# Grouped attention: the last two steps divide the probabilities before the product with the values, and the last output weights take another place and another time

## The reference, cut to what matters

```
q = rmsnorm((x @ q_proj.T) by head);  k = rmsnorm((ctx @ k_proj.T) by group);  v = ctx @ v_proj.T by group
scores = q @ k.T * scale + mask
attn = softmax(scores)            # exp(scores - max) / sum
out = (attn @ v) by head
x = x + out @ o_proj.T
```

## Time and profile before

| | |
|---|---|
| median of three runs | 867.71 us (864.17 to 871.29) |
| profiled execution | 866.43 us, of which the span from first to last instruction is 864.3 us |
| busy share of the span | PE 90%, DVE 83%, ACT 60%, POOL 48% |
| mean granted clock of PE | 0.974 |
| step 14 by PE's units | 711.5 to 744.5 us of the span |
| step 15 with its tail | 744.5 to 783.2 us |

### The profile page before, as it was taken

How to read it: one execution, slowest core, us unless ns; L and a number is a source line. 1 busy time by engine, 2 the same in 40 slices (tenths; PEclk the granted TensorE clock), 3 DMA queues, 4 the chain that set the end, 5 groups by cost and what they waited for, 6 DMA issues and landing times. The chain is left out here.

```text
span 864.3 us, 16319 instructions
## 1 busy us (share of the span) xinstructions
PE 779.7 (90%) x5146; PEld 631.4 (73%) x5146; DVE 715.1 (83%) x1743; ACT 522.2 (60%) x1414; POOL 415.8 (48%) x372
## 2 busy tenths in 40 slices
PE   1976799858988999999999999999999999788878
PEld 0475577534677898898898888888888888675446
DVE  7877998969787887887897897897897897787975
ACT  6875798745556657557557657657657556551521
POOL 3237068715036745845744845745746645511110
PEclk9998999979999999999999999999999999899989
DMA  8255236544020310310220220320220220003001
GB/s 300 101 164 155 73 123 229 173 126 149 26 74 21 119 35 20 97 54 3 94 73 0 97 73 0 97 73 0 97 73 0 74 75 1 26 1 119 0 1 49
DMA packets 37775, 66.20 MB, mean 77 GB/s; under 512 B 5537, under 2 KB 17889, under 8 KB 37602
## 3 DMA queue, kind: packets, MB, share of 16 engines
q1 hardware_dynamic: 37730, 65.63, 23.2%
HBM read 60.28 MB, written 5.34 MB: 76 GB/s over the span
## 5 line engine op out<-in xcount | busy, mean ns | idle before, releaser
L2377 DVE TENSOR_SCALAR_CACHE_REDUCE xn<-ctxT,candidate 128x512 bf16<-128x512 f32 x240 | 168.8, 741 | 0.0
L2029 ACT ACTIVATE layer_attention_probs<-xnT,stats 128x512 f32<-128x512 f32 x128 | 93.9, 734 | 123.2 <-DVE stats L2172 123.2
L1764 PE MATMUL bank<-layer_attention_keysT,layer_attention_queriesT 128*128 128x512 f32 x384 | 121.9, 426 | 5.0 <-DVE layer_attention_queriesT L2165 5.0
L2184 DVE TENSOR_TENSOR layer_attention_probsT<-bank,layer_attention_probsT 128x512 fp32r<-128x512 f32 x128 | 88.1, 688 | 44.7 <-ACT layer_attention_probsT L2037 43.2
L1764 PEld LDWEIGHTS bank<-layer_attention_probsT,layer_attention_values 128*128 128x128 f32 x768 | 99.6, 190 | 13.4 <-DVE layer_attention_probsT L2184 6.0
L1764 PE MATMUL bank<-layer_attention_probsT,layer_attention_values 128*128 128x256 f32 x768 | 102.4, 283 | 5.1 <-DVE layer_attention_probsT L2184 5.1
L2037 ACT CAST layer_attention_probsT<-bank 128x512 fp32r<-128x512 f32 x128 | 74.9, 585 | 52.3 <-PE bank L1840 48.4
L1764 PE MATMUL bank<-layer_attention_l_wq,layer_attention_xnT 128*128 128x512 f32 x384 | 93.5, 392 | 0.0
L1764 PEld LDWEIGHTS bank<-layer_attention_l_wkv,layer_context_parts 128*128 128x128 f32 x720 | 88.5, 188 | 2.8
L1764 PE MATMUL bank<-layer_attention_l_wkv,layer_context_parts 128*128 128x256 f32 x720 | 90.5, 278 | 0.0
L1764 PE MATMUL bank<-layer_attention_wo,layer_attention_headsT 128*128 128x512 f32 x336 | 88.8, 406 | 0.0
(11 more groups left out here) (338 smaller groups left out, 1717.7 us busy)
## 6 DMA issues: line engine op xcount, KB each, us to landing
layer_attention_l_raw_qo<-in_wqT SPq DMA_DIRECT2D x8, 1024.0 KB, 5.5
layer_attention_l_raw_qo<-in_woT SPq DMA_DIRECT2D x8, 1024.0 KB, 6.5
xnT<-inverse_sums SPq DMA_DIRECT2D x15, 512.0 KB, 3.8
tw_raw<-in_w_gateT SPq DMA_DIRECT2D x8, 688.0 KB, 5.2
tw_raw<-in_w_upT SPq DMA_DIRECT2D x8, 688.0 KB, 4.3
tw_raw<-in_w_downT SPq DMA_DIRECT2D x6, 768.0 KB, 4.7
layer_attention_l_raw_kv<-in_wkvT SPq DMA_DIRECT2D x8, 512.0 KB, 4.8
ternary<-tw_rounded SPq DMA_DIRECT2D x8, 344.0 KB, 2.5
```

The costliest lines, as they stand in the source:

```text
L1764: last = pe.matmul(out, stationary[f][a], moving[f][b], start=f == 0 and x == 0, stop=f == count - 1 and x == 2)
L2029: a.activation(probs[:, u % 3, :], masked[:, u % 2, :], ACT.Exp, bias=negmax[:, u:u + 1], scale=-1.0, accum_out=sums[:, u:u + 1]).then_inc ...
L2184: v.tensor_tensor(probsT[:, 1, p % 2, :, columns], T[u % 2][:, :].rearrange("p (c q) -> p c q", c=CPB), probsT[:, 0, p % 2, :, columns], A ...
L2377: own(k.nc.vector.tensor_scalar((k.flags if flags is None else flags)[:, r % 2], row_tile(k.ctxT, r), k.candidate[:, r:r + 1].bitcast(F32) ...
```

## The change

Step 14 is made like step 15: the sums are inverted by unit on DVE, ACT scales each unit's probabilities, and the heads are split by ACT and DVE; the spread through DRAM and POOL's scale_heads of step 14 are gone. The split heads of both steps and the last output weights take halves of the context parts (ctxT2) that no later product reads. The last output weights are split earlier: ACT's halves stand after u 3 and 4, and POOL's halves on either side of norm(15, KEYS), as in odd steps. In step 15 the output product of step 14 is spread in quarters over u 1, 3, 5 and 6, where it stood at u 4 and 5 in halves; the last product runs by row block over three heads, and the fourth head after the last mix. DVE's pieces of the choice and its additions move by a unit or so. The functions last_turn, last_mix, last_heads_high, last_heads_low and last_invert are merged into the general ones.

```diff
-    FINAL_PIECES = (1, 1, 1, 1, 1, 1, 1, 1)
+    FINAL_PIECES = (1, 2, 1, 2, 1, 1, 1, 1)
...
-        last_inverse = k.sbuf("last_inverse", [P, UNITS], F32, s)
-        last_headsT, last_wo = xnT2, wq
+        last_inverse = k.sbuf("last_inverse", [P, 2 * UNITS], F32, s)
+        last_wo = ctxT2[:, :, :, 0:D]
...
+        def divided(step):
+            return step[0] is None and step[1] >= STEPS - 2
+
+        def divided_heads(step):
+            return ctxT2[:, :, :, D + step[1] % 2 * SEQ:D + (step[1] % 2 + 1) * SEQ]
...
 sync:    run((None, STEPS - 3), weights=False)
-                run((None, STEPS - 2))
...
 gpsimd run():
-                    if odd:
+                    if odd or not weights:
                         o_weights_low(step, 0)
                     norm(following, own, KEYS)
-                    if odd:
+                    if odd or not weights:
                         o_weights_low(step, 1)
                     norm(following, own, 0)
...
-                    elif not odd:
-                        o_weights_low(step, 0)
-                        o_weights_low(step, 1)
...
-                for j in range(2):
-                    scale_heads((None, STEPS - 2), j)
...
 tensor, turn_probs():
-                    pe.wait_ge(S_["exp_ready"], at(step, UNITS, u + 1))
+                    if divided(step):
+                        pe.wait_ge(S_["probs_scaled"], divided_unit(step, u + 1))
+                    else:
+                        pe.wait_ge(S_["exp_ready"], at(step, UNITS, u + 1))
...
 tensor, run_final():
+                        if u == 1:
+                            project_out(before, 0, 0)
                         if u == 2:
-                            last_mix(0)
+                            mix(final, 0)
+                        if u == 3:
+                            project_out(before, 0, 1)
                         if u == 4:
-                            last_mix(1)
-                        if u in (4, 5):
-                            project_out(before, u - 4, 0)
-                            project_out(before, u - 4, 1)
+                            mix(final, 1)
+                        if u == 5:
+                            project_out(before, 1, 0)
                         if u == 6:
-                            last_mix(2)
-                    last_project_out(0)
-                    last_project_out(1)
-                    last_mix(3)
-                    last_project_out(2)
-                    last_project_out(3)
+                            mix(final, 2)
+                            project_out(before, 1, 1)
+                    last_project_out(0, (0, 1, 2))
+                    mix(final, 3)
+                    last_project_out(1, (0, 1, 2))
+                    last_project_out(0, (3,))
+                    last_project_out(1, (3,))
...
 scalar:
+                def scale_probs(step, u):
+                    a.wait_ge(S_["inverted"], divided_unit(step, u + 1))
+                    a.activation(probs[:, u % 3, :], probs[:, u % 3, :], ACT.Copy,
+                                 scale=last_inverse[:, divided_unit(step, u):divided_unit(step, u) + 1])\
+                     .then_inc(S_["probs_scaled"], 1)
...
 scalar run():
-                        if u in (3, 6, 7):
+                        if u in (3, 6, 7) and divided(step):
+                            divided_heads_high(step, (3, 6, 7).index(u))
+                        elif u in (3, 6, 7):
                             copy_mixed(step, (3, 6, 7).index(u))
-                        if u + 1 < UNITS:
-                            exponentials(step, u + 1)
-                        else:
-                            exponentials(following, 0)
+                        coming = (step, u + 1) if u + 1 < UNITS else (following, 0)
+                        exponentials(*coming)
                         probsT_high(step, u)
+                        if divided(coming[0]):
+                            scale_probs(*coming)
...
-                        if not odd and not weights and u in (5, 6):
-                            last_o_weights_high(u - 5)
+                        if not odd and not weights and u in (3, 4):
+                            last_o_weights_high(u - 3)
...
 vector:
+                def divided_heads_low(step, p):
+                    heads = divided_heads(step)
+                    v.wait_ge(S_["last_high"], divided_pair(step, p + 1))
+                    v.tensor_tensor(heads[:, 1, p], mixed_bank(step, p), heads[:, 0, p], ALU.subtract)\
                      .then_inc(S_["last_low"], 1)
...
 vector run():
-                        if u == UNITS - 1:
+                        if u == UNITS - 1 and not divided(step):
                             invert(step)
...
+                        if divided(step) and u in (3, 6, 7):
+                            divided_heads_low(step, (3, 6, 7).index(u))
...
+                        coming = (step, u + 1) if u + 1 < UNITS else (following, 0)
+                        if divided(coming[0]):
+                            divided_invert(*coming)
                     if not first:
                         add_out(before, 1)
...
 vector run_final():
-                        if u in (4, 6):
-                            last_heads_low(u // 2 - 2)
-                        if u in (6, 7):
-                            add_out(before, u - 6)
+                        if u == 1:
+                            divided_heads_low(before, PAIRS - 1)
+                        if u in (4, 6, 7):
+                            divided_heads_low(final, (4, 6, 7).index(u))
+                        if u in (5, 7):
+                            add_out(before, (5, 7).index(u))
```

More of the change, by code:

```diff
@@ L1798, in project_out @@
                 def project_out(step, t, half, drained=None):
+                    heads = divided_heads(step) if divided(step) else headsT
                     if t == 0:
                         pe.wait_ge(S_["o_low"], 2 * group(step) + half + 1)
+                    if t == 0 and divided(step):
+                        pe.wait_ge(S_["last_low"], divided_pair(step, half * 2 + 2))
+                    elif t == 0:
                         pe.wait_ge(S_["heads_low"], headed(step, half + 1))
@@ L1807, in project_out @@
                     last = product(J[t][:, :],
-                                   [[headsT[:, a, h, token:token + P] for a in range(2)] for h in range(REP)],
+                                   [[heads[:, a, h, token:token + P] for a in range(2)] for h in range(REP)],
                                    [[wo_of(step)[:, x, h, :] for x in range(2)] for h in range(REP)], half)
@@ L1844, in mix @@
                 def mix(step, p):
-                    if not is_start(step) or p >= 1:
+                    if divided(step) and divided_pair(step, p):
+                        pe.wait_ge(S_["last_low"], divided_pair(step, p - (1 if step[1] == STEPS - 2 or p == 0 else 2) + 1))
+                    elif not is_start(step) or p >= 1:
                         pe.wait_ge(S_["mix_copied"], at(step, PAIRS, p))
                     pe.wait_ge(S_["probsT_low"], at(step, UNITS, 2 * p + 2))
-                    product(V[:, 0:SEQ],
+                    product(mixed_bank(step, p),
                             [[values[:, a, batch(step) * CPB + c, :] for a in range(2)] for c in range(CPB)],
@@ L1895, in run @@
                             turn_rows(following, TURNS[u - 4])
[L1897 to L1914, removed]
@@ L1916, in last_project_out @@
-                def last_project_out(h):
-                    if h == 0:
-                        pe.wait_ge(S_["o_low"], 2 * GROUPS)
-                        pe.wait_ge(S_["out_added"], added(after(final, -1), TPB))
-                    pe.wait_ge(S_["last_low"], h + 1)
-                    for t in range(TPB):
+                def last_project_out(t, last_heads):
+                    heads = divided_heads(final)
+                    if t == 0 and 0 in last_heads:
+                        pe.wait_ge(S_["o_low"], 2 * GROUPS)
+                    if 0 in last_heads:
+                        pe.wait_ge(S_["out_added"], added(after(final, -1), t + 1))
+                    for h in last_heads:
+                        if t == 0:
+                            pe.wait_ge(S_["last_low"], divided_pair(final, h + 1))
@@ L1930, in run_final @@
                     for u in range(UNITS):
-                        last_turn(u)
+                        turn_probs(final, u)
                         if u + 2 < UNITS:
@@ L2059, in o_weights_high, with divided_heads_high @@
                     a.copy(wo[:, 0], raw_o[:, :, :]).then_inc(S_["o_high"], 1)
+                def scale_probs(step, u):
[3 more added lines that the diff above has]
+                     .then_inc(S_["probs_scaled"], 1)
+                def divided_heads_high(step, p):
+                    a.wait_ge(S_["mix_psum"], at(step, PAIRS, p + 1))
```

(1 more changed line is left out.)

49 lines of the change are left out of this document (21 added, 28 removed).

## The result

The changed kernel is slightly slower: 869.17 us (median of 20 runs) where the kernel before has 864.90 (20 runs in the same sessions). The ratio is 1.0046, with a 95% interval of 1.0028 to 1.0063. I had predicted 872.7 against 867.7, a ratio of 1.0058. The profiled execution took 868.48 us, its span 865.9.

What follows compares the result with a forecast made beforehand. PE was taken as the bound, busy throughout step 14, then waiting on DVE's queue at the seam. The terms +0.56 + 8.0 + 2.2 - 3.4 - 1.5 - 0.9 = +5.0 us gave 872.7 us, range 866 to 878.

Steps and rivals of the forecast that it cites:

- Step 2, the keys: In step 14 PE waits at the keys of step 15 for POOL's norm, queued behind low output weights: +8.0 us.
- Rival A: No wait at the keys, because POOL's order doesn't act as read: 862.5 us; chance 0.12.
- Step 3, the clock: Behind the wait at the keys PE runs at half clock: +2.2 us, bounds 0 and 4.4.
- Rival B: Clock slow for twice the stretch after the keys' wait and falling again at the seam: 877.8 us; chance 0.15.
- Step 4, the seam and unit 1: From step 14's last scores to step 15's first transposes: -3.4 us; on to unit 1's transposes: -1.5 us.
- Step 4, step 15: From second to last transposes of step 15, quarters fill PE's gaps: -0.9 us, bounds -3.3 and +1.5.
- Step 1, the start of step 14: Unit 0's transposes at the start of step 14 wait for reciprocal and scaling: +0.56 us.
- Rival C: ACT becomes the bound of step 14 through its added scalings: +3 us, 875.7 us; chance 0.05.

Runs made afterwards that it cites:

- e1: Changed kernel with POOL norming the keys and first queries of step 15 ahead of the low output weights: 861.77 us, ratio 0.9961 to the kernel before.
- e3: Changed kernel with ACT's two halves of the last high output weights after u 0 and 1 instead of 3 and 4: 862.42 us, ratio 0.997.
- e6: Kernel before with only the changed placement of the last output weights, POOL's halves on either side of the keys' norm: 869.38 us, ratio 1.0046.
- e2: Changed kernel with 30 dummy products on PE ahead of its wait for the normed keys of step 15: 866.53 us, ratio 1.0022.
- e5: Changed kernel with DVE's reciprocal for unit 0 of step 14 ahead of the bisection's update: 869.61 us, ratio 1.006.
- e7: Changed kernel with the diffs of e1 and e5 together: 862.02 us, ratio 0.9964 to the kernel before.
- e8: Kernel before with the last output weights in the context half, POOL's halves after the norms of the first and second queries: 860.78 us, ratio 0.9952.
- e4: Kernel before with only step 14's output product in quarters after u 1, 3, 5 and 6 of step 15: 864.13 us, ratio 0.999.
- e9: Kernel before with the moved weights of e8 and the quarters of e4, step 14 undivided: 858.1 us, ratio 0.9932.

## Why the prediction was right, step by step

The sum was +5.0 us and the local sum of the two profiles is +5.20. The ratio measured, times 867.7, is +4.0 us. That the two sums meet within 0.2 us is in part luck: +1.4 us at the start of step 14, from a collision that I hadn't foreseen and that three of the eleven profiled kernels show, stand against -0.4 at the keys, -0.5 in step 15 and -0.3 at the end.

- **Step 2, the keys: right.** Predicted +8.0, measured +7.63 between the first transposes of step 14 and the keys. The idle time is 7.51 us. e1 removes it by POOL's order alone, e3 by ACT's signal alone, and e6 brings it about without the rest of the change. Rival A is refuted. My working has a slip: three scalings and the 0.56 are 2.4 us, and with the 0.34 of the head subtraction the update ends at 729.0, not 728.5, which makes the wait 8.5. Counted from the anchor I had the scaling of unit 4 at 18.4 us; it began at 18.1 in e2, where nothing was held up at the start, and at 19.5 in the changed kernel.
- **Step 3, the clock: right in size.** Predicted +2.2, measured +2.27; e2 shows 1.75 of them to be the clock. The size varies: behind waits of 7.5 and 5.8 us the stretch is longer by 1.7 in e5 and 1.8 in e6. Rival B didn't occur here: the clock stayed up at the seam. The point from which I let it decide, a gap near 3 us, was too high: in the changed kernel the clock fell 2.0 us into the wait, and in e7 a gap of 2.33 us was enough. A fall at the seam cost 0.9 us there, not the 2.2 that I gave it.
- **Step 4, the seam and unit 1: right.** Predicted -3.4 and -1.5, measured -3.43 and -1.52, with the pieces at 0.87 and 0.76 us. The explanation, POOL beside DVE's pieces, is borne out by e8, where moving the weights (their place, ACT's halves and POOL's) closes the seam without the division and without the quarters. The Trainium skill's rule, page "SBUF — State Buffer", section "SBUF: two separate sides", is that a DVE instruction with two SBUF inputs and a GpSimd instruction that reads SBUF shut each other out: the one that starts first has the shared ports to its end, the other waits. The trace agrees: in e3 POOL's instruction ends at 730.58 and the small one on DVE at 730.60.
- **Step 4, step 15: mis-sized by 0.5.** Predicted -0.9, measured -1.43 with -0.27 more at the end. e4 shows that the quarters alone give more than that (-1.85, and +0.34 at the end).
- **Step 1, the start of step 14: mis-sized.** I gave +0.56 and it was +1.95. Without the collision it is +0.57 (e1), so the term as I worked it out was right, and what I missed is that the reciprocal stands behind an update which POOL's scaling can hold up by 1.4 us. The trace of the kernel before has the pair of rows for it: the update's last instruction begins at 712.30 and POOL's scaling at 712.54. I looked for collisions only where they had happened.
- **Rival C: absent as a bound in the changed kernel, but seen once the wait is gone.** In e1 ACT works without a pause and step 14 loses 1.6 us behind the keys. The long wait had hidden that, as I wrote. The 1.8 us of e3 are another thing: DVE held up by POOL.

What I didn't see is that the removal of POOL's scaling, the main part of the change, isn't needed for any of its gain. I credited the seam to the pieces being free of POOL altogether. e8 shows that moving the weights alone frees them. Comparing e9 with e1, which differ by the division in step 14 (and in the order of the last product and of DVE's pieces), the division costs about 2.2 us local, 1.6 of them behind the keys.

## What to carry to other kernels

When an instruction is moved ahead of others on an in-order engine, ask first what it waits for, and then who needs what is now behind it. Here a product whose result was wanted 20 us later stood in front of a norm wanted at once. Two engines that block each other in memory belong in the same question: look up what the other one runs at the new place, and at every place where they pass within half a microsecond, for POOL's start at the one place varied by 0.43 us over eleven kernels. And when a change has three parts, time them apart: one of these cost 0.5%, and another gave more without its neighbour.

## What the runs showed of the hardware

A DVE instruction over 8 columns took 1.54 us in place of 0.17 because a POOL instruction had begun 0.05 us before it; where POOL began 0.08 us after it (e7), it took 0.17. That is a coin thrown by the landing of a DMA, worth 1.3 to 1.4 us of the local sum. Beside a POOL instruction of 2.38 us such a small one took 2.30 (e3), so the partner's length counted and not its own. The granted clock fell to 0.50 after 2.0 us of idle in the changed kernel and stayed at 1.00 through a gap of 2.29 (e1), so the length of a gap alone doesn't tell. The slow products behind it cost 0.9 us in e7 (4.13 in place of 3.20). A comparison of one input with a scalar was held up beside POOL as the instructions with two inputs were (2.63 us for two, in place of 0.61).
